# The first node stage writes the second convolution's table parts itself

## The reference, cut to what matters

```python
m = (x * dout[:, None])[src]
agg = segment_sum(m, dst, num_segments=N)
h = agg * din[:, None] @ W + b          # done twice: W1, b1, then W2, b2 on h
x = layernorm(x + h)
x = layernorm(x + edge_network(x, ...)) # untouched here
```

## Time and profile before

| | |
|---|---|
| median of 3 runs | 7610.92 us |
| the profiled execution, its own time | 7614.77 us |
| its span, first to last instruction | 7612.9 us |
| PE busy | 6617.5 us (87%) |
| DVE busy | 4748.7 us (62%) |
| ACT busy | 3399.5 us (45%) |
| POOL busy | 4890.6 us (64%) |
| mean granted clock of PE | 0.872 of 2.4 GHz |

### The profile page before, as it was taken

The page is one execution under the profiler, slowest core; times in us unless marked ns, Lnnn a source line. Parts: engine busy times, 40 slices in busy tenths (PEclk is TensorE's granted clock), DMA queues, the critical chain, the costliest instruction groups (busy, mean ns, idle before and its releaser), DMA issues.

```text
span 7612.9 us, 125645 instructions
## 1 busy us (share of the span) xinstructions
PE 6617.5 (87%) x37688; PEld 5566.4 (73%) x37689; DVE 4748.7 (62%) x9176; ACT 3399.5 (45%) x6948; POOL 4890.6 (64%) x4864
## 2 busy tenths in 40 slices
PE   6899987999987999986888888888888888888887
PEld 4666656888876888875777777777777777777776
DVE  9999984333334333337666666666666666666665
ACT  5999974555545555543222222222222222222322
POOL 2211103777774777774777777777777777777775
PEclk9999999999999999998777777777777778787876
DMA  3666556555545555544223333233233333333331
GB/s 81 131 133 131 125 121 188 162 167 167 166 136 167 166 167 167 167 140 138 83 85 85 84 84 85 84 85 85 84 85 84 84 85 84 84 85 84 85 84 55
DMA packets 604288, 868.26 MB, mean 114 GB/s; under 512 B 217478, under 2 KB 470461, under 8 KB 599025
## 3 DMA queue, kind: packets, MB, share of 16 engines
q0 software_dynamic: 158000, 437.63, 22.0%
q1 hardware_dynamic: 419980, 414.21, 19.2%
q10 hardware_dynamic: 26036, 12.80, 0.6%
HBM read 706.91 MB, written 157.30 MB: 114 GB/s over the span
## 4 chain that ended last, share of the span: by engine, by line
POOL 34%; issue 13%; DMA 3%; DVE 2%; POOLq 1%; DVEq 0%; SPq 0%; PE 0%; ACT 0%; ACTq 0%
POOL t_rows L1758 34%; DMA t_rows<-table,t_ends 2%; DMA t_attrs<-in_edge_attr 1%; DVE t_msg_ad L2022 1%; POOLq L179 0%; DVE t_msg_bc L2036 0%; DVE t_cg L2021 0%; SPq L1730 0%; DVE t_msg_ad L2024 0%; POOLq L1756 0%; DVE t_ge L2018 0%; DVE t_rel L2109 0%; DVE acc L1999 0%; DVE t_msg_bc L2031 0%; DVEq L2120 0%
## 5 line engine op out<-in xcount | busy, mean ns | idle before, releaser
L1758 POOL DMA_INDIRECT t_rows<-table,t_ends x3224 | 3048.0, 945 | 1005.5 <-issue 967.7
L1035 POOL DMA_INDIRECT c_early<-table,c_first_src x1408 | 1559.0, 1107 | 661.3 <-issue 452.7
L1937 PEld LDWEIGHTS t_sums<-t_hot,t_msg_ad 128*128 128x128 f32 x6464 | 952.0, 232 | 922.5 <-issue 921.6
L1779 ACT ACTIVATE t_weight<-t_weight,t_attrs 128x64 f32<-128x64 f32 x3224 | 691.9, 302 | 2092.1 <-PE t_weight L1880 2084.0
L1125 ACT ACTIVATE c_wide_act<-c_raw 128x1024 fp32r<-128x1024 uint8 (+1 forms) x1120 | 1160.0, 1039 | 880.1 <-PE c_sums L1269 876.7
L1937 PE MATMUL t_sums<-t_hot,t_msg_ad 128*128 x6464 | 986.5, 318 | 619.7 <-DVE t_hot L2116 618.2
L1204 DVE CAST c_wide_dve<-c_raw 128x1024 fp32r<-128x1024 uint8 (+1 forms) x1120 | 653.2, 585 | 1257.1 <-PE c_sums L1269 1256.2
L1269 PE MATMUL c_sums<-c_wide_act,c_parts 128*128 128x512 f32 (+1 forms) x4480 | 1213.3, 394 | 72.8 <-DVE c_parts L1188 62.3
L2018 DVE TENSOR_TENSOR t_ge<-t_rows,t_edge 128x768 f32<-128x768 f32 x403 | 384.7, 955 | 1207.3 <-DMA t_rows<-table,t_ends 1196.2
L1940 PE MATMUL t_sums<-t_hot,t_msg_bc 128*128 x6464 | 1090.3, 341 | 0.0
L1940 PEld LDWEIGHTS t_sums<-t_hot,t_msg_bc 128*128 128x128 f32 x6464 | 1054.3, 255 | 0.0
(11 more groups left out here) (240 smaller groups left out, 6778.9 us busy)
## 6 DMA issues: line engine op xcount, KB each, us to landing
c_raw<-a_dram SPq DMA_DIRECT2D x532, 448.0 KB, 3.5
a_dram<-a_a_sb POOLq DMA_DIRECT2D x39, 3136.0 KB, 18.2
t_scal<-in_edge_attr SPq DMA_DIRECT2D x403, 256.0 KB
t_rows<-table,t_ends POOLq DMA_INDIRECT x3224
c_early<-table,c_first_src POOLq DMA_INDIRECT x1408, 3.1
t_ends<-in_edges SPq DMA_DIRECT2D x403, 8.0 KB
t_attrs<-in_edge_attr SPq DMA_DIRECT2D x403, 16.0 KB
c_raw<-a_dram SPq DMA_DIRECT2D x28, 224.0 KB, 2.6
```

Source lines behind the costliest of these rows:

```text
L1035: pool.indirect_dma_start(out=rows_of_group[:, q % 2, t], out_offset=None, in_=table_of_rows, in_offset=bass.IndirectOffsetOnAxis(ap=c.fir ...
L1758: pool.indirect_dma_start(out=rows[:, slot, t, :], out_offset=None, in_=table, in_offset=bass.IndirectOffsetOnAxis(ap=ends[:, slot, t:t + ...
L1779: mul = act.activation(ad, ad, ACT.Copy, scale=attrs[:, slot, t, 0:1])
L1937: pe.matmul(sums[:, of, 0:WIDE], msg_ad[:, slot % 2, t, :], hot[:, of, t, :], start=t == 0, stop=t == T - 1)
```

## The change

The tensor `parts` now outlives c1: it is made in `gnn_kernel`, around c1, the first node stage and c2. In the first node stage DVE masks each step's rows (the new buffer `n1_lead`) and writes the subtraction into `parts`; ACT copies the mask's result into `parts`, one step behind its copies out of `acc`. The last step first clears the block that has 84 rows only. c2 no longer loads its table, masks, copies or subtracts, and PE waits for no part. `table_1` is still stored, for the gathers. In c2 the first group is due after step 1 instead of step 15, and POOL starts gathering at once. c1 works as before.

```diff
@@ convolve_counts
-            q, rest = divmod(n - NHC - 1, STEPS_OF_N)
+            q, rest = divmod(n - first_group, STEPS_OF_N)
...
+        first_group = 1 if scaled is None else NHC + 1
...
             def _(pool):
-                pool.wait_ge(part1, NHC)
-                pool.wait_ge(part0, NHC)
                 if scaled is not None:
+                    pool.wait_ge(part1, NHC)
+                    pool.wait_ge(part0, NHC)
...
-                    if n < NHC:
+                    if scaled is not None and n < NHC:
                         load_x(n)
...
-                    if n < NHC:
+                    if scaled is not None and n < NHC:
                         take_lead(n)
...
-                        if s == 0:
+                        if s == 0 and scaled is not None:
                             pe.wait_ge(part0, i + 1)
                             pe.wait_ge(part1, i + 1)
@@ first_nodes, ACT
                                    ACT.Copy).then_inc(agg_ready, 1)
+                    if later(i, 1):
+                        take_lead(i - 1, (b + 1) % 2, QB)
+
+                def take_lead(i, b, k):
+                    act.wait_ge(lead_ready, i + 1)
+                    act.activation(parts[:, 0, bass.ds(i * QB, k), :], lead[:, b, 0:k].bitcast(F32), ACT.Copy
+                                   ).then_inc(part0, 1)
                 node_steps(act, body)
+                take_lead(NQ, NQ % 2, NB - NQ * QB)
@@ first_nodes, DVE
+                    if blocks[-1] < P:
+                        dve.wait_ge(part1, i - 1)
+                        dve.memset(out[:, b, len(blocks) - 1], 0.0).then_inc(cleared, 1)
+                        dve.wait_ge(cleared, 1)
                     dve.wait_ge(bias_ready, i + 1)
                     dve.wait_ge(prod_ready, i + 1)
...
                     last.then_inc(made, 1)
+                    k = len(blocks)
+                    if later(i, 2):
+                        dve.wait_ge(part0, i - 1)
+                        dve.wait_ge(part1, i - 1)
+                    dve.wait_ge(made, i + 1)
+                    dve.tensor_scalar(lead[:, b, 0:k], out[:, b, 0:k].bitcast(I32), LEADING, None, ALU.bitwise_and
+                                      ).then_inc(lead_ready, 1)
+                    dve.wait_ge(lead_ready, i + 1)
+                    dve.tensor_tensor(parts[:, 1, bass.ds(i * QB, k), :], out[:, b, 0:k], lead[:, b, 0:k].bitcast(F32),
+                                      ALU.subtract).then_inc(part1, 1)
@@ gnn_kernel
+                with nc.sbuf_tensor("parts", [P, 2, HI, D], F32R) as parts:
+                    convolve_counts(nc, c, "c1", x, a_dram, edges, bounds_dram, acc, parts, table_0)
+                    first_nodes(nc, c, acc, table_1, parts)
+                    convolve_counts(nc, c, "c2", table_1, a_dram, edges, bounds_dram, acc, parts)
```

More of the change, by code:

```diff
@@ L938, in _, with convolve_counts @@
                 act.activation(root[:], least[:], ACT.Sqrt).then_inc(root_ready, 1)
-def convolve_counts(nc, c, name, table, a_dram, edges, bounds_dram, acc, scaled=None):
+def convolve_counts(nc, c, name, table, a_dram, edges, bounds_dram, acc, parts, scaled=None):
     ctx = ExitStack()
@@ L958, in convolve_counts @@
         hot = early[:, 2 * T * D:2 * T * D + T * WIDE].rearrange("p (t w) -> p t w", t=T)
-        parts = sb("parts", [P, 2, HI, D], F32R)
         raw = sb("raw", [P, ASLOTS, 2, HCH, BLK], U8)
@@ L1006, in group_after @@
         def group_after(n):
-            q, rest = divmod(n - NHC - 1, STEPS_OF_N)
+            q, rest = divmod(n - first_group, STEPS_OF_N)
             return q if rest == 0 and 0 <= q < SG else None
         table_of_rows = table if scaled is None else scaled
-        assert NHC + 2 + (SG - 1) * STEPS_OF_N < NSPAN * NHC
+        first_group = 1 if scaled is None else NHC + 1
+        assert first_group + 1 + (SG - 1) * STEPS_OF_N < NSPAN * NHC
         def widen(n, unit):
@@ L1056, in load_x @@
                         sp.wait_ge(part1, i - (XSLOTS - 1))
-                        if scaled is not None:
-                            sp.wait_ge(kept[slot], rows_of_slot(i - XSLOTS))
+                        sp.wait_ge(kept[slot], rows_of_slot(i - XSLOTS))
                     if i == NHC - 1:
@@ L1093, in take_lead @@
                     slot = i % XSLOTS
[L1094 to L1097, removed]
+                    act.wait_ge(ready, i + 1)
+                    for p, s, to in rows(scaled, i):
+                        act.dma_start(to, x[p, slot, s]).then_inc(kept[slot], 16)
                     act.wait_ge(lead_ready, i + 1)
@@ L1140, in make_few_hot @@
                 def make_few_hot(q):
-                    if q == 0:
+                    if q == 0 and scaled is not None:
                         dve.wait_ge(part0, NHC)
@@ L1165, in scale @@
                             dve.wait_ge(part1, i - (XSLOTS - 1))
-                            if scaled is not None:
-                                dve.wait_ge(kept[slot], rows_of_slot(i - XSLOTS))
+                            dve.wait_ge(kept[slot], rows_of_slot(i - XSLOTS))
                         dve.memset(x[:, slot, HCH - 1, :], 0.0).then_inc(cleared, 1)
                     dve.wait_ge(x_landed[slot], rows_of_slot(i))
[L1170 to L1173, removed]
+                    dve.tensor_tensor(x[:, slot], x[:, slot],
+                                      c.dout[:, i * HCH:(i + 1) * HCH, None].to_broadcast([P, HCH, D]), ALU.mult
+                                      ).then_inc(ready, 1)
                 def take_lead(i):
@@ L1177, in take_lead @@
                         dve.wait_ge(cleared, 1)
-                    if scaled is not None:
-                        dve.wait_ge(ready, i + 1)
+                    dve.wait_ge(ready, i + 1)
                     if i >= 1:
@@ L1189, in take_rest @@
                                       ALU.subtract).then_inc(part1, 1)
-                scale(0)
+                if scaled is not None:
+                    scale(0)
                 for n in range(NSPAN * NHC):
-                    if n < NHC:
+                    if scaled is not None and n < NHC:
                         take_lead(n)
@@ L1294, in _, with first_nodes @@
                         pe.reg_add(visits, visits, 1)
-def first_nodes(nc, c, acc, table):
+def first_nodes(nc, c, acc, table, parts):
     ctx = ExitStack()
@@ L1303, in first_nodes @@
         out = ctx.enter_context(nc.sbuf_tensor("n1_out", [P, 2, QB, D], F32))
+        lead = ctx.enter_context(nc.sbuf_tensor("n1_lead", [P, 2, QB, D], I32))
         prod = [ctx.enter_context(nc.psum_tensor(f"n1_prod{b}", [P, QB, D], F32)) for b in range(2)]
-        agg_ready, prod_ready, bias_ready, made = [
-            ctx.enter_context(nc.semaphore("n1_" + n)) for n in ("agg_ready", "prod_ready", "bias_ready", "made")]
+        agg_ready, prod_ready, bias_ready, made, cleared, lead_ready, part0, part1 = [
+            ctx.enter_context(nc.semaphore("n1_" + n)) for n in ("agg_ready", "prod_ready", "bias_ready", "made",
+                                                                 "cleared", "lead_ready", "part0", "part1")]
         stored = [ctx.enter_context(nc.semaphore(f"n1_stored{i}")) for i in range(2)]
@@ L2193, in gnn_kernel @@
             with nc.sbuf_tensor("acc_0", [D, NB + 1, P], F32) as acc:
-                convolve_counts(nc, c, "c1", x, a_dram, edges, bounds_dram, acc, table_0)
-                first_nodes(nc, c, acc, table_1)
-                convolve_counts(nc, c, "c2", table_1, a_dram, edges, bounds_dram, acc)
+                with nc.sbuf_tensor("parts", [P, 2, HI, D], F32R) as parts:
+                    convolve_counts(nc, c, "c1", x, a_dram, edges, bounds_dram, acc, parts, table_0)
+                    first_nodes(nc, c, acc, table_1, parts)
+                    convolve_counts(nc, c, "c2", table_1, a_dram, edges, bounds_dram, acc, parts)
                 second_nodes(nc, c, x, acc, x1_dram, table_2)
```

## The result

The kernel after takes 7597.55 us in the median of 14 runs (7587.46 to 7601.43), the kernel before 7610.62 (14 runs, 7606.5 to 7620.05); the ratio is 0.9981, 95% interval 0.9973 to 0.9989. That is 13.1 us less where I had forecast 22.5 less. The time lies inside the range, 9.2 us above the forecast, but outside A's own 7582 to 7596, and inside the 7597 to 7607 of rival D. The interval excludes 1, but the gain is 0.19%, just short of the 0.2% from which I had counted a time as faster. A ratio here is not the quotient of the two medians (that would be 0.9983); the two differ by up to 0.0004, or 3 us, so a timed difference between two variants is no better than that.

What follows compares the result with a forecast made beforehand. PE bounds the second convolution's middle, its own stores the node stage. Profiled 7614.8 - 37.3 (convolution) + 14.8 (node stage) = 7592.3, and 3.9 lower on the timed runs' scale: 7588.4 us; range 7582 to 7614.

Steps and rivals of the forecast that it cites:

- A: Whole kernel: the forecast itself, 7588 us, own range 7582 to 7596, DVE not held by POOL; chance 0.50.
- rival D: Node stage: part of B, some holds or half of POOL's time; 7597 to 7607, taken at 7600; chance 0.12.
- Start of the second convolution: Second convolution: a raw load comes first instead of a table load, first matmul at 5.0 instead of 7.8; saves 2.8 us.
- First span and groups' place: Second convolution: chunks 0 to 14 at PE's pitch save 25.8 us; groups moved earlier save 20.4 - 7.7 = 12.7.
- Rival C: Second convolution's first span stays as slow, paced by raw loads, not table loads; 7614 us; chance 0.05.
- Tail: Second convolution's end: last addition 12.9 us after the last chunk instead of 8.9; 4.0 given back.
- Node stage: First node stage: DVE's added work makes a step 2.54 us instead of 1.94; costs 14.8 over 24 steps.
- the hidden store: First node stage: two steps of DVE (5.1 us) exceed the store's circle of 3.87, so DVE becomes the bound.
- the third gap: First node stage: the last of three gaps of 0.10 us in DVE's step sum of 2.54.
- B: Node stage: POOL holds the port for 1.04 us between mask and subtraction; step 3.58, kernel 7613; chance 0.33.
- ACT's circle: Node stage: ACT's copies with PE at half clock take 3.3 us from mask to second next addition, DVE 3.4; hidden.

Runs made afterwards that it cites:

- groups_late: Kernel after with the second convolution's groups beginning after the first span, as before the change: 7615.80 us, ratio 0.9991 to the kernel before.
- bias_late: Kernel after with POOL's bias in the node stage waiting for the subtraction of two steps earlier instead of the additions: 7594.20 us, ratio 0.9965.
- two_behind: bias_late with ACT's copy of the mask's result two steps behind instead of one: 7592.52 us, ratio 0.9959 to the kernel before.
- bias_twice: Kernel after with a second POOL product of the same size, into a spare buffer, ahead of the bias: 7604.87 us, ratio 0.9976.
- again: Kernel after, unedited, run and profiled once more: 7605.96 us against 7622.96 for the kernel before, ratio 0.9975.
- list_early: bias_late with SP loading the last group's list right behind the first span's raw loads: 7590.01 us, ratio 0.9952 to the kernel before.

## Why the prediction was right or wrong

**Start of the second convolution.** Forecast 2.8 saved, measured 1.8: first matmul 2337.65 - 2331.57 = 6.1 after the first load, 7.8 before. ACT's widening begins 5.0 after that load, not 3.5; the median of the earlier trace rows is too short for it. That three such loads were issued close together may be why; this was not tested.

**First span and groups' place.** The first span alone took 47.2 in groups_late, 46.8 forecast and 72.6 before: 25.4 saved of 25.8. In the kernel after, from the first matmul to the last span, it is 3352.53 - 2337.65 = 1014.9 us against 1033.7 before: 18.8 saved, forecast 25.8 - 7.7 = 18.1. That the two agree to 0.7 is partly luck, since the same stretch takes 1044.8 and 1036.1 in the two other profiles without the change. PE at its pitch was what came late next, and chunk 0 at the lower clock took 2343.55 - 2337.65 = 5.9, near the 2.4 + 3.2 forecast. The last span takes 3376.21 - 3352.53 = 23.7 (23.5 forecast) and saves 20.2. Rival C, raw loads as the pace, falls: PE waited for none in either kernel. groups_late prices the moved groups by themselves.

**Tail.** 3388.43 - 3376.21 = 12.2 after the last chunk, forecast 12.9; 3.3 given back instead of 4.0. Sum: 1.8 + 18.8 + 20.2 - 3.3 = 37.5, as the stage's 37.4 (bounds 33 to 40). With the repeats it is 36.0 to 45.3 (1094.0 and 1101.9 before, 1056.6 and 1058.0 after).

**Node stage: the step that failed.** I had put the subtraction at the 0.69 of the earlier trace rows, on the ground that nothing in the trace showed POOL delaying DVE. It measures 1.28 while POOL's bias runs, and 0.69 without it (bias_late). The step is 3.04 instead of 2.54; (3.04 - 1.94) x 24 = 26.4 against 26.1 measured. That term was 0.59 short, 14.2 in 24 steps. Of the rest of the sum the mask (0.43 for 0.42) and the hidden store held; the two waits on its own results took 0.14 and 0.16 for 0.10 each, and the third gap is not there: the next additions are recorded 0.07 before the subtraction's end. A step with no overlap and no wait is so 2.47, not 2.54 (two_behind). Altogether the stage was forecast 11.3 too cheap, and that is the whole error: 22.5 - 11.3 = 11.2, timed 13.1. I gave B 0.33 and D 0.12; it was D. That the time still lies in the range is due to the range, which took in the rivals: the forecast's own mechanism failed in this stage.

What I chose wrongly was the evidence. L1146 meets gathers, which POOL issues, and that says nothing on POOL's arithmetic. I also misread the gather of the earlier trace rows: 1.53 us is not the price of meeting L1146, for it went on into a cast, a row that I had not shown:

```profile
2607.40 0.69 DVE L1204 CAST c_wide_dve<-c_raw 128x1024 fp32r<-128x1024 uint8 x1
```

The gather ends at 2608.20, 0.11 after that cast. From 2450 to 3300 of the trace of before, 81 gathers that met no DVE work took 0.94 us in the median, 72 that began during an L1146 took 0.99, and 199 that began during such a cast took 1.39. So it was the casts, with one input, that held gathers up in this trace, and L1146, with two, hardly did.

**Why D and not B.** B put POOL's 1.04 whole between mask and subtraction. But `made` releases both at once, and POOL's operation, stretched by only 0.23, was recorded from 0.05 after the mask's start; just 0.74 us of it (2273.08 to 2273.82) were left when the subtraction came. The Trainium skill ("SBUF — State Buffer", section "SBUF: two separate sides") gives a DVE operation that runs in a two-port mode or has two SBUF inputs, and a GpSimd operation, which has to read SBUF if DVE has the two inputs, a shared port pair with an exclusive lock, held for an instruction by whoever starts first. The rows agree for the subtraction, which has two inputs: it gets on when POOL's operation ends, at 2273.82, needs 0.54 more, and in bias_twice it does so ahead of POOL's next. The mask has one input, so the rule would reach it only in a two-port mode, which no run here shows by itself; but the mask and POOL do hold each other up, the later one each time. Begun 0.05 before POOL, the mask stays at 0.43 and POOL is stretched; begun 0.05 after it, at 2324.20, the mask takes 0.84.

That it is a lock and not a sharing is seen in the ends, which are the same however long the two overlap (one touch of 0.02 us aside). In the traces of after, again, groups_late and bias_twice the held subtraction ends 0.54 to 0.56 after POOL's operation (recorded with 1.28 or 1.41), the held product 0.88 to 0.90 after the mask or the subtraction (recorded with 1.16, 1.27 or 1.48), the held mask 0.28 or 0.29 after the product. Each is the operation's own 0.69, 1.04 or 0.43, less about 0.15. What the rule does not give, and bias_twice does, is that a new POOL operation does not pass a waiting DVE.

**PE.** I had ACT's circle "hidden, closely", with 2.0 for PE at half clock. It was hidden at 3.04 a step and not at 2.47: the mean step of bias_late is 2.64, and two_behind, which opens the circle, takes 2.46. That the clock would fall from 0.83 to 0.52, and PE's matmuls of a step take 2.07 us (PE waits about 1 us in each step), I had as a bound and not as the expected case. Over the stage the clock was 0.83 at a step of 1.94, 0.63 at 2.46 (two_behind), 0.55 at 2.64 (bias_late) and 0.52 at 3.04; the two go together here, and no run tells which moves the other.

## What to carry to other kernels

When work is added to DVE, look at what work of POOL the same semaphore releases: arithmetic on both at once made DVE's subtraction 0.59 us longer in nearly every step, and one changed wait took that back. A row that shows one kind of POOL work (a gather) harmless to DVE does not speak for another kind (arithmetic); where no row shows the pair, the bound belongs in the likeliest case if the order of release makes them meet in every step. And when a late stage gets shorter, look for the loads issued last: here the last group's list, issued at 3370.36, left some 9 us in the open, and in list_early, where it is issued at 2378.41, the tail is 9.1 us shorter.

## What the runs showed of the hardware that I had not expected

Beside POOL's 128x512 product DVE's subtraction of that size goes from 0.69 to 1.28, but its additions out of PSUM stay at 1.12 and leave the product at 1.04 (bias_late). A product that begins just behind the mask takes 1.27. Two operations that hold each other up do not share: in four traces the later one ended at a fixed time after the earlier one's end, its own lone duration less about 0.15 us. The first convolution, the same instructions on the same data, took 1106.5 to 1117.9 us over the twelve profiles, a scatter of 11.4 us, nearly as large as the timed gain of 13.1: a stage's cost has to be read in that stage, not from two spans.
